# Placing the causal row maxima by TensorE's column counts, and a seventh product of parts

## The reference, cut to what matters

```python
# L1_attn_a: windows of 128 queries over all keys up to the window's end; the mask leaves
# the first 128 keys as a triangle per window
scores = einsum('bhqd,bhkd->bhqk', wq, wk) * scale
scores = where(mask, neg, scores); attn = softmax(scores); out = attn @ wv
# L1_ffn (used twice): causal attention, then a mixture of experts
att = einsum('bhqd,bhkd->bhqk', q, k) / sqrt(hd)
att = where(tril, att, -inf); att = softmax(att); y = att @ v
```

## Time and profile before

| What | us |
|---|---|
| Median of 3 executions (2479.47 to 2480.95) | 2479.57 |
| Profiled execution, its own time | 2487.47 |
| Its span, first to last instruction | 2485.8 |
| TensorE busy in the span | 2003.1 (81%) |
| VectorE busy | 1615.8 (65%) |
| ScalarE busy | 1413.1 (57%) |
| GpSimd busy | 862.5 (35%) |
| Mean granted TensorE clock | 0.893 of full |

### The profile page before, as it was taken

One profiled execution on the slowest core, in us unless ns is written; L12 is line 12 of the kernel. 1 busy time (PEld: TensorE's weight loads), 2 busy tenths in 40 slices (PEclk: granted clock), 3 DMA queues, 4 the chain that ended last, 5 costly groups with the idle time before them and its releaser, 6 DMA issues. The chain is left out here.

```text
span 2485.8 us, 37632 instructions
## 1 busy us (share of the span) xinstructions
PE 2003.1 (81%) x13700; PEld 1133.4 (46%) x13700; DVE 1615.8 (65%) x3493; ACT 1413.1 (57%) x2024; POOL 862.5 (35%) x554
## 2 busy tenths in 40 slices
PE   4999999999999944858835786688879745888798
PEld 3566666666666632622232533222236622222367
DVE  5887787877877546651156464788723586888424
ACT  3777776777768643269853244366654152566641
POOL 3787776877768500242201202211100013111100
PEclk7999999999999966969957888599989865899899
DMA  2000000000000040062050111211010002210100
GB/s 78 1 5 1 4 5 1 1 3 5 1 3 1 1 144 29 2 161 54 16 174 1 43 51 48 70 27 28 15 35 1 1 0 66 70 34 15 35 1 18
DMA packets 53859, 77.56 MB, mean 31 GB/s; under 512 B 13150, under 2 KB 21422, under 8 KB 53550
## 3 DMA queue, kind: packets, MB, share of 16 engines
q1 hardware_dynamic: 53678, 75.16, 11.0%
HBM read 56.16 MB, written 18.22 MB: 30 GB/s over the span
## 5 line engine op out<-in xcount | busy, mean ns | idle before, releaser
L831 ACT ACTIVATE probs<-psum_banks 128x1024 f32<-128x1024 f32 (+1 forms) x416 | 384.3, 980 | 245.2 <-PE psum_banks L668 200.2
L1263 POOL TENSOR_SCALAR l0a_rows<-l0a_rows,l0a_rinv 128x1024 f32<-128x1024 f32 x160 | 454.5, 2846 | 190.4 <-DVE l0a_rinv L1225 186.8
L911 DVE TENSOR_REDUCE neg_max<-psum_banks 128x1 f32<-128x512 f32 (+3 forms) x672 | 414.1, 660 | 122.2 <-PE psum_banks L720 99.1
L1213 DVE TENSOR_REDUCE l0a_nmax<-psum_banks 128x1 f32<-128x1024 f32 x256 | 312.4, 1220 | 140.3 <-PE psum_banks L1107 138.3
L1159 ACT ACTIVATE l0a_rows<-psum_banks,l0a_nmax 128x1024 f32<-128x1024 f32 x256 | 286.0, 1117 | 62.6 <-DVE l0a_nmax L1213 61.2
L854 POOL TENSOR_SCALAR_AFFINE_SELECT probs<-probs 128x512 f32<-128x512 f32 x192 | 124.1, 651 | 531.4 <-ACT probs L831 470.3
L691 PE MATMUL psum_banks<-probs,v_ones 128*32 128x512 f32 (+3 forms) x2432 | 267.6, 523 | 4.5 <-POOL probs L854 4.3
L1121 PE MATMUL psum_banks<-packed,l0a_rows 128*128 128x128 f32 x2048 | 267.1, 273 | 2.7 <-POOL l0a_rows L1263 1.6
L1106 PE MATMUL psum_banks<-l0a_kh,l0a_qw 128*128 128x512 f32 x512 | 242.9, 474 | 21.8 <-POOL l0a_qw L1252 13.9
L1121 PEld LDWEIGHTS psum_banks<-packed,l0a_rows 128*128 128x128 f32 x2048 | 239.2, 141 | 43.0 <-issue 5.3
L713 PE MATMUL psum_banks<-k_stack,q_stack 48*128 48x128 bf16 (+3 forms) x1024 | 144.9, 335 | 136.5 <-DVE neg_max L911 103.9
(11 more groups left out here) (289 smaller groups left out, 3358.1 us busy)
## 6 DMA issues: line engine op xcount, KB each, us to landing
q_stack<-q_parts SPq DMA_DIRECT2D x74, 96.0 KB
qkv<-in_l0f_w SPq DMA_DIRECT2D x6, 1024.0 KB, 5.5
k_stack<-k_eight SPq DMA_DIRECT2D x28, 192.0 KB
k_eight<-parts SPq DMA_DIRECT2D x20, 256.0 KB
moe_b<-in_l0f_b SPq DMA_DIRECT2D x32, 128.0 KB, 3.7
k_stack<-k_eight SPq DMA_DIRECT2D x16, 256.0 KB
l1f_w<-in_l1f_w SPq DMA_DIRECT2D x16, 256.0 KB
q_stack<-q_parts SPq DMA_DIRECT2D x58, 64.0 KB
```

Of the source, the lines that this page charges most:

```text
L831: act.activation(S.Pt[:, U % PBUFS, 2 * half:2 * half + 2, c0:HALF], PS[:, bank:bank + 2, c0:HALF], ACT.Exp).then_inc(exp_done, 1)
L911: dve.tensor_reduce(out, scores, AX, ALU.max, negate=True).then_inc(job_read, 1)
L1213: dve.tensor_reduce(R.nmax4[:, s % 4:s % 4 + 1], scores(s), AX, ALU.max, negate=True).then_inc(max_done, 1)
L1263: rows_divided.mark(pool.tensor_scalar(R.Pr[:, s % RING, :], R.Pr[:, s % RING, :], R.rinv4[:, s % 4:s % 4 + 1], None, ALU.mult))
```

## The change

1. A seventh product of parts (second key part with third query part): the stacks hold 56 rows of products and 59 with the maximum. One more copy of a key part is stored, so 10 stores instead of 9, and one load of a query part grows from two parts to three.
2. `spread` places a group's pairs by a running sum of columns instead of by steps: each step has three places (behind `cols(U, 0)`, behind `values`, behind `cols(U, 1)`), each place costs the columns of the product ahead of it, with 4 times the width plus 460 for the values, and a pair goes to the place whose sum is nearest to its due share. A place may hold two pairs or none.
3. A turn now stands behind the values (second place) of its step in the causal attention; divides always stand in the third place. In steps without pairs a turn or divide stood in the first places before.
4. `split_shift` becomes a function that any engine could run; VectorE still runs it. The minimum over the halves (L866) signals a semaphore of its own. Two semaphores are added to the phase, of which one (`pool_split`) is not used.

```diff
-    copies = ((0, 1, 2), (3, 4), (5,)) if use_max else ((0, 1, 2), (3, 4, 5), (6, 7))
+    copies = ((0, 1, 2), (3, 4, 5), (6,)) if use_max else ((0, 1, 2), (3, 4, 5), (6, 7))
...
-    products_of, rows_of_stack, per_batch = (48, 51, 144) if use_max else (64, 64, 176)
-    parts_of_q = ((0, 3), (24, 2), (40, 1)) if use_max else ((0, 3), (24, 3), (48, 2))
+    products_of, rows_of_stack, per_batch = (56, 59, 160) if use_max else (64, 64, 176)
+    parts_of_q = ((0, 3), (24, 3), (48, 1)) if use_max else ((0, 3), (24, 3), (48, 2))
...
+EARLY, TURN = 3, 3
+def column_costs(units):
+    shape_change = 460
+    costs = []
+    for side, kt, c0 in units:
+        w = HALF - c0
+        cols = [2 * w, 0] if w <= HALF // 2 else [w, w]
+        costs.append((cols[0], 4 * w + shape_change, cols[1]))
+    return costs
...
-    steps = [[] for _ in range(ng * nu + LAG + 5)]
+    steps = [([], [], []) for _ in range(ng * nu + LAG + 5)]
+    costs = column_costs(units)
     def spread(events, s0, n):
+        places, done = [], 0
+        for s in range(s0, s0 + n):
+            first, values, second = costs[(s - 1) % nu][0], costs[(s - 1 - LAG) % nu][1], costs[(s - 1) % nu][2]
+            for place, cost in enumerate((first, values, second)):
+                if cost:
+                    done += cost
+                    places.append((done, s, place))
         for k in range(0, len(events), 2):
-            steps[s0 + k * n // len(events)] += events[k:k + 2]
+            due = (k + 1) * done / len(events)
+            _, s, place = min(places, key=lambda x: abs(x[0] - due))
+            steps[s][place].extend(events[k:k + 2])
...
-                late = 2 if g == lead else -3
-                spread(jobs, s0 + late, nu - 3 - late)
-                steps[s0 + nu - 3].append(whole)
+                late = 2 if g == lead else -EARLY
+                spread(jobs, s0 + late, nu - EARLY - late)
+                steps[s0 + nu - TURN][1].append(whole)
...
-            steps[1 + g * nu + last_unit(units, side) + LAG + 1].append(("divide", g, side))
+            steps[1 + g * nu + last_unit(units, side) + LAG + 1][2].append(("divide", g, side))
...
-                side_work(items[:1] if use_max else ())
+                side_work(places[0])
                 if use_max and 0 <= U - LAG < total:
                     values(U - LAG)
...
-                side_work(items[1:2] if use_max else ())
-                if U < total and not narrow(U):
+                side_work(places[1])
+                if 0 <= U < total and not narrow(U):
                     cols(U, 1)
-                side_work(items[2:] if use_max else items)
+                side_work(places[2])
...
+        def join_halves(dve, e):
+            dve.wait_ge(job_read, last_rows[e] + 1)
+            if 1 in e[2] and nk(NT - 1) > 1:
+                later = S.nmax[:, e[1] % 2, :, 4:8]
+                dve.tensor_tensor(later, later, S.nmax[:, e[1] % 2, :, 8:12], ALU.min).then_inc(joined, 1)
...
-                                split_shift(t)
+                                join_halves(dve, t)
+                                if joins(t):
+                                    dve.wait_ge(joined, joins(t))
+                                split_shift(dve, own, t)
```

More of the change, by code:

```diff
@@ L279, in _ @@
                 if split:
[L280 removed]
+                    sp.wait_ge(stored, 16 * 10)
         @block.tensor
@@ L525, in four_heads @@
     lead = 0 if not use_max else 2 if nu < 4 else 1
-    steps = side_jobs(ng, nu, nk, use_max, lead)
-    order = [e for events in steps for e in events]
+    steps = side_jobs(ng, units, nk, use_max, lead)
+    order = [e for places in steps for events in places for e in events]
     number = {e: n for n, e in enumerate(order)}
@@ L764, in side_job, with side_work @@
                 m.then_inc(job_ready, 1)
[L766 to L769, removed]
-                    else:
-                        side_job(item[0])
-            for s, events in enumerate(steps):
+            def side_work(events):
+                left = list(events)
+                while left:
+                    if left[0][0] == "rows":
+                        score_pair(left[:2])
+                        left = left[2:]
+                    else:
+                        side_job(left[0])
+                        left = left[1:]
+            for s, places in enumerate(steps):
                 U = s - 1
[L775 to L781, removed]
+                if 0 <= U < total:
                     cols(U, 0)
-                side_work(items[:1] if use_max else ())
+                side_work(places[0])
                 if use_max and 0 <= U - LAG < total:
@@ L804, in evict, with joins, split_shift @@
                     eng.tensor_copy(S.Oc[:, out % 2, :], PS[:, 7, :]).then_inc(evicted, 1)
+        def join_halves(dve, e):
[3 more added lines that the diff above has]
+                dve.tensor_tensor(later, later, S.nmax[:, e[1] % 2, :, 8:12], ALU.min).then_inc(joined, 1)
+        def joins(e):
+            return sum(1 in t[2] and nk(NT - 1) > 1 for t in turns[:turn_at[e] + 1])
+        def split_shift(eng, own, e):
+            k, g, sides = turn_at[e], e[1], e[2]
+            if k >= 2:
+                eng.wait_ge(c_copied, k - 1)
+            x = S.nmax[:, g % 2, :, 4 * sides[0]:4 * sides[-1] + 4]
+            x = x.rearrange("p (k i) j -> p i k j", i=2)
+            out = S.cs[:, k % 2, 0:48 * len(sides)]
+            out = (out.rearrange("p (i a k j) -> p a i k j", i=2, a=3, k=2) if len(sides) == 2
+                   else out.rearrange("p (i k a j) -> p a i k j", i=2, a=3, k=2))
+            for a in range(2):
+                own.link(eng.tensor_copy(out[:, a], x))
+                own.link(eng.tensor_tensor(x, x, out[:, a], ALU.subtract))
+            eng.tensor_copy(out[:, 2], x).then_inc(c_split, 1)
         @block.scalar
```

26 lines of the change are left out of this document (13 added, 13 removed).

## The result

The changed kernel takes 2508.39 us (median of 4, 2502.63 to 2514.49) against 2480.26 (median of 4) before: ratio 1.0101, interval 1.0078 to 1.0125. It is slower, as forecast, but by 28 us and not by 7, and outside the range. Its profiled execution takes 2509.08 us, with a span of 2507.4, 21.6 more than the span before. The other 6.5 us of the 28 are in no comparison of these two traces: the kernel before was traced in an execution of 2487.47, 7.2 above its median. I take the spans apart.

What follows compares the result with a forecast made beforehand. VectorE, which reads the row scores, was taken to set the causal attention. Two causal blocks +6.8, layer 1's attention a -0.4 and stores +1.7 gave +8 on the median 2479.57: 2487 us, range 2474 to 2495.

Steps and rivals of the forecast that it cites:

- the starvation: Steady causal groups: VectorE runs dry where ScalarE's exponentials set the pace; its idle grows from 3.3 to 3.84 us a group.
- +0.57 a period: Steady causal groups: the new order of pairs lengthens each group by 0.57 us, bounds -2.7 to +2.5.
- the walk: One causal group stepped through with the trace's durations: 28.76 us in the old order (28.74 measured), 29.33 in the new.
- Stretches A and B: Two parts of a causal group set by ScalarE's exponentials, 4.13 and 2.42 us, keeping their length while pairs move out.
- the new semaphores change nothing: Minimum over the halves: its link was waited for before as well, on the same engine, so no cost.
- five periods run at full clock with both orders: Steady groups of a causal block: five periods at full clock, 0.57 us more each, +2.9 us a block.
- The rival of the clock: Causal blocks' first groups: TensorE's clock rises later, 3.6 us for two blocks or 12.6 more, 2491 to 2500; chance 0.06.
- First groups: Start of each causal block, at the lower clock: the new order costs +0.8 us, between -0.1 and +1.2.
- Attention a: Layer 1's attention a: shorter waits -2.0, shape changes +0.4, two added store costs of +0.6 each; together -0.4 us.
- Stores ahead of a block: Passage before each causal block: 256 KB more stored delays TensorE's first columns by 0.85 us, two blocks +1.7.
- Divides and turns: Causal groups: divides behind the second columns add one product-shape change a group, +0.7 us a block, between 0 and 2.9.
- Block ends: End of each causal block: last pair and divides later among values and columns, -1.0 us, between -1.5 and 0.

Runs made afterwards that it cites:

- two other orders: Changed kernel with causal pairs due a quarter of a pair later, 2494.7 us; or with steady groups' pairs in places chosen from computed durations, 2479.4 us.
- the order by hand: Changed kernel, steady causal groups' pairs in places chosen from computed durations, GpSimd's select behind the split: 2475.4 us with seven products, 2477.4 with six.

## Why the prediction was wrong, point by point

**Right: the starvation.** +0.57 a period was forecast from 28.76 to 29.33. With the select out of the way the period is 29.35 (0.1 of it for divides and turns), with the last pair moved 29.27, and with two other orders the walk stood within 0.1 once the select's 0.5 is added or taken out (28.55 for 28.03 + 0.5; 28.4 for 27.8 + 0.5, and 27.90 for 27.8 with the select moved). Stretches A and B are held by ScalarE as told, from 1685.54 to 1689.65 (4.11 us) and from 1695.95 to 1698.38 (2.43), and VectorE's idle before the first full reductions of key blocks 4 and 6 is 0.65 and 0.66, forecast at about 0.7:

```profile
1689.65 0.11 PEld L691 LDWEIGHTS psum_banks<-q_stack,k_stack 59*128 59x128 bf16 x4 [0.60 <-ACT probs L874]
...
1698.37 0.10 PEld L691 LDWEIGHTS psum_banks<-q_stack,k_stack 59*128 59x128 bf16 x2 [0.82 <-ACT probs L874]
```
```profile
1690.30 2.65 DVE L938 TENSOR_REDUCE neg_max<-psum_banks 128x1 f32<-128x512 f32 x4 [0.65 <-PE psum_banks L736]
...
1699.02 2.65 DVE L938 TENSOR_REDUCE neg_max<-psum_banks 128x1 f32<-128x512 f32 x4 [0.66 <-PE psum_banks L736]
```

**Wrong: +0.57 as the whole price of a steady period, from a walk of columns, values, pairs, reductions and exponentials.** That is the first step that failed: GpSimd's select is not in the walk, so the split kept its old length there. But the new place of the last pair puts the split beside the select, and VectorE waits: 0.48 in the minimum in eight of the ten later periods, 0.32 in the first cast in the other two, 4.5 us. The sentence that the new semaphores change nothing is not what failed: they are still there in the runs where the minimum takes 0.18.

**Wrong: "five periods run at full clock with both orders".** That is the second step, and the dearest. The rival of the clock was set in each block's first groups and priced at 3.6 us, chance 0.06. The lower clock came in the steady groups, which ran at 1.00 before. There the new order leaves TensorE nothing while VectorE splits: the last pair stands one value product later, so the products that filled that time have already run. Seven of ten later periods lose 1.4 to 1.5 against a period without a drop (29.83, or 29.67 where the cast is held), 10.4 in all. Doubled quads, which only give TensorE something to do there, remove every drop: shown. With 6.0 for starvation, divides and turns (29.35 against 28.75, ten times) and 4.5 for the select, that is the 20.9 of the table.

**Both prices stood in the trace of before.** The earlier trace rows shows only the minima. In the first two groups of both blocks the split does meet a select, and one operation behind the minimum takes 0.49 to 0.51; in the steady groups the select starts only with the split's last cast. Block 2's second group shows the clock too: TensorE waits 0.99 and 0.78, is then granted 0.55, and the period is 30.51 us (2135.73 to 2166.24), where block 1's second, with waits of 0.76 and 0.78 and 1.00 granted, is 29.06:

```profile
2135.73 0.68 POOL L854 TENSOR_SCALAR_AFFINE_SELECT probs<-probs 128x512 f32<-128x512 f32 x1 [22.15 <-ACT probs L831]
```
```profile
2135.94 0.50 DVE L873 CAST c_split<-neg_max 128x32 bf16<-128x32 f32 x1
```
```profile
2138.06 0.39 PE L713 MATMUL psum_banks<-k_stack,q_stack 48*128 48x256 bf16 x4 [0.99 <-DVE neg_max L911]
...
2140.13 0.50 PE L713 MATMUL psum_banks<-k_stack,q_stack 48*128 48x256 bf16 x4 [0.78 <-DVE neg_max L911]
```
```profile
2140.00:2143.00 3.00, 2.87 (x18) 0.78 (x20) 1.40 (x3) 0.60 (x1) 1.02 (x2) 0.55 0.04 8
```

**The kernel's spread** (2502.6 to 2514.5) would follow if the number of groups that drop differs between executions; only one was traced, so this is argued.

**First groups:** forecast +0.8 a block, measured -1.3 and -0.4 for the first period. The order isn't what decides there: with the old order and the seventh product the same period was 31.5, and 34.4 with the tenth store, against 35.04 in the earlier trace rows (block 1). Its granted clock differs from run to run, 0.83 after against 0.56 in the earlier trace rows:

```profile
1592.00:1621.40 29.40, 20.67 (x171) 6.44 (x165) 23.70 (x45) 14.81 (x17) 4.95 (x4) 0.83 0.41 122
```

**Attention a:** forecast -0.4, measured about -1.4: the work ahead of it to its start 0.5 longer (the store, forecast 0.6), and from ScalarE's first work in the stage (0.7 us earlier than before) to its first behind it (2.6 earlier) 1.9 shorter. It ends 2.9 earlier, where within 1 us was forecast. The waits went as told. TensorE's turn and its last divide after (before, the turn waited 0.57 and each of the last two divides, 1510.45 in the earlier trace rows and 1512.88, waited 0.81):

```profile
1496.38 0.26 PE L781 MATMUL psum_banks<-ident_b,c_split 128*96 128x128 bf16 x1
...
1510.02 0.63 PE L786 MATMUL psum_banks<-packed,o_sum 128*128 128x128 f32 x4 [0.21 <-ACT o_sum L822]
```

Its last divide starts at 1510.02 where the old one started at 1512.88, with the turn level: the last two sides overlap, 2.8 us where I had 1.4 for both.

**Stores ahead of a block:** forecast 0.85 each. Six stores, 1.57 MB, now take 82.5% of 6.1 us (1537.7 to 1543.8): 0.84 each. ScalarE's first work in the two blocks falls back by 0.9 each against its work before them.

```profile
q1 hardware_dynamic: 862, 1.57, 82.5%
```

**Divides and turns:** forecast 0.7 a block; with the pairs by step 0.1 a period, 1.0 over the ten later ones.

**Block ends:** forecast -1.0 each, measured -0.1: from the last minimum to the last divide 27.58 us before (1794.22 to 1821.80) and 27.44 after (1800.21 to 1827.65). The last turn waits 1.88 us for the split where it waited 1.28.

**Open:** the seventh product, or the tenth store alone, made the kernel before 8 to 9 us slower by the medians, where the trace shows 2.4, and in the order by hand it does not. Single traces can't settle this: the kernel before was traced in an execution 7 us above its median, and the tenth store's trace is 5 us shorter than that one, while its median is 8.7 longer. And the 5 us behind the second block, in code that is the same: 61 to 76 us into that piece TensorE is granted 0.77 after and 1.00 before. Over the thirteen traces the piece takes 175.4 to 177.2 us in eight and 180.6 to 181.1 in five, with the old places of pairs and with new ones in either (181.1 with the seventh product, 175.8 with the tenth store alone), so these 5 us are not shown to come from the change. Both look like the clock falling elsewhere when all later work is shifted by a few us, but no run here holds the shift and varies nothing else.

## What to carry to other kernels

A hand-made or computed order has to be judged by what else stands beside a step at its new time, not by its own length: walk the order through with the durations, then ask of each moved instruction what GpSimd does just then, and of TensorE where it will have nothing queued. The price of either may stand in the trace already, in groups that run otherwise than the steady ones. Even spacing by columns was no goal in itself: the same rule with due times a quarter of a pair later gained 1.3 us a group where nothing dropped (29.83 to 28.55), and moving one pair in nineteen gained 1.6 (30.84, the mean of the ten later periods, to 29.27). Where TensorE must idle in a dense stretch, a useless product can cost less than the clock: 0.65 us of it took 10 us off the ten later periods.

## What the runs showed of the hardware that was not expected

The granted clock fell after two waits of TensorE with products between them, the second 0.78 us in all of these. With a first wait of 1.16 or 0.99 it fell in 7 of the 10 later groups of the changed kernel and in 6 of 10 with the pairs a quarter later, with 0.94 and with 0.68 in 4 of 10, with 0.49 or 0.22 in none. What decides between groups with the same waits is not shown. A group in which it falls is 1.5 us longer than its neighbour (31.35 and 29.83).

A GpSimd select of 0.64 us held a two-input VectorE operation on 16 elements a partition for 0.48 us and a cast for 0.26 to 0.32, but not a reduction.
